# Attention prologues of a four-block Flamingo kernel: order of loads and queries, bias cleaned per pair, two PSUM banks

## The reference

```
x = x + tanh(g_xattn[i]) * attention_i(layernorm(x), ctx)
q = norm_x @ Wq.T (+ bq);  k = ctx @ Wk.T (+ bk);  v = ctx @ Wv.T (+ bv)
first attention:  q, k, v = nan_clamp(...)      # NaN -> 0, +inf -> 1e4, -inf -> -1e4
                  bias = clip(nan_clamp(bias), -1e4, 1e4)      # (1, 16, 56, 1500), same for all sequences
                  logits = q.k / sqrt(8) + bias; where mask == 0: -1e4; softmax; @ v; @ Wo.T + bo
second attention: softmax(q.k / sqrt(8)) @ v @ Wo.T             # no biases, no mask
fourth attention: softmax(q.k / sqrt(8) - 1e6 * mask) @ v @ Wo.T + bo
```

## Time and profile before

| | |
|---|---|
| median of 3 runs | 6163.29 us |
| profiled execution | 6152.64 us, span 6150.5 us, mean granted clock 0.936 |
| busy in the span | PE 86%, VectorE 73%, ScalarE 52%, GpSimd 30% |
| first attention, its first DMA to its first VectorE scores | 19.88 to 163.91 us |
| second attention, its first DMA to the matmul on the context of sequence 2 | 1646.79 to 1738.40 us |
| fourth attention, the same | 4962.67 to 5056.78 us |

### The profile page before, as it was taken

The page is one execution under the profiler, slowest core; times in us unless marked ns, Lnnn a source line. Parts: engine busy times, 40 slices in busy tenths (PEclk is TensorE's granted clock), DMA queues, the critical chain, the costliest instruction groups (busy, mean ns, idle before and its releaser), DMA issues. The chain is left out here.

```text
span 6150.5 us, 133121 instructions
## 1 busy us (share of the span) xinstructions
PE 5287.2 (86%) x51447; PEld 3802.1 (62%) x51447; DVE 4466.4 (73%) x9168; ACT 3193.4 (52%) x6024; POOL 1844.2 (30%) x1456
## 2 busy tenths in 40 slices
PE   1888989888669999989839999999999749999997
PEld 1777777777258888877824444444444427888885
DVE  6898898986357777763457777777777547777776
ACT  0666666666246666652224444444444216666663
POOL 4777676772022222211001111111111022222220
PEclk6999999999689999999969999999999869999998
DMA  4555565553167777743010000000000048888981
GB/s 107 124 131 126 127 129 125 131 125 80 37 122 140 140 140 139 140 81 115 24 31 21 16 15 15 15 15 15 15 15 10 7 91 151 163 161 161 161 155 30
DMA packets 368544, 545.53 MB, mean 89 GB/s; under 512 B 115780, under 2 KB 248006, under 8 KB 367606
## 3 DMA queue, kind: packets, MB, share of 16 engines
q1 hardware_dynamic: 365894, 533.81, 42.9%
q0 software_dynamic: 2048, 3.67, 0.2%
HBM read 413.45 MB, written 123.90 MB: 87 GB/s over the span
## 5 line engine op out<-in xcount | busy, mean ns | idle before, releaser
L653 DVE CUSTOM_DVE_ANT_0 attn_logits<-attn_scores,attn_shift 112x750 f32<-112x750 f32 x1024 | 944.9, 932 | 440.3 <-PE attn_scores L457 440.0
L569 ACT ACTIVATE attn_probs_t<-attn_pt 125x448 f32<-125x448 f32 x1536 | 829.6, 541 | 581.7 <-PE attn_pt L472 561.1
L472 PEld LDWEIGHTS attn_pt<-ident,attn_logits 112*125 112x125 f32 x6144 | 851.6, 189 | 179.7 <-issue 92.8
L472 PE MATMUL attn_pt<-ident,attn_logits 112*125 112x112 f32 x6144 | 920.7, 273 | 26.4 <-ACT attn_logits L560 24.8
L2246 PE MATMUL attn2k_pk<-attn_wk,attn2k_cn_t 128*125 128x512 f32 x1536 | 738.8, 603 | 53.0 <-ACT attn2k_cn_t L2317 36.7
L2257 PE MATMUL attn2k_pg<-attn2k_kn,attn2k_cn 125*128 125x512 f32 x1536 | 725.0, 594 | 6.0 <-ACT attn2k_gram L2325 3.9
L2412 DVE TENSOR_REDUCE attn2k_ss<-attn2k_sq 125x16 f32<-125x1024 f32 x384 | 466.9, 1216 | 257.7 <-ACT attn2k_sq L2354 257.6
L386 POOL CAST attn_k_parts<-xn_t 128x500 bf16<-128x500 f32 x192 | 199.3, 1038 | 1422.6 <-DVE xn_t L623 1422.6
L2354 ACT ACTIVATE attn2k_sq<-attn2k_pk 125x1024 f32<-125x1024 f32 x384 | 391.5, 1019 | 324.8 <-PE attn2k_pk L2246 324.6
L1165 ACT ACTIVATE attn_probs_t<-attn_pt 125x448 f32<-125x448 f32 x768 | 413.8, 539 | 275.0 <-PE attn_pt L1053 273.0
L2246 PEld LDWEIGHTS attn2k_pk<-attn_wk,attn2k_cn_t 128*125 128x125 f32 x1536 | 273.1, 187 | 416.7 <-issue 320.8
(11 more groups left out here) (363 smaller groups left out, 10434.9 us busy)
## 6 DMA issues: line engine op xcount, KB each, us to landing
attn_k_packed<-k_scratch SPq DMA_DIRECT2D x384, 375.0 KB, 6.4
attn_k_packed<-k_scratch SPq DMA_DIRECT2D x384, 187.5 KB, 4.4
k_scratch<-attn_k_parts SPq DMA_DIRECT2D x64, 1125.0 KB, 7.6
attn_ctx_t<-in_ctx_t SPq DMA_DIRECT2D x64, 750.0 KB, 7.4
k_scratch<-attn_k_parts SPq DMA_DIRECT2D x96, 375.0 KB, 3.7
attn_ctx_t<-in_ctx_t SPq DMA_DIRECT2D x96, 250.0 KB, 4.1
attn2k_ctx<-in_ctx SPq DMA_DIRECT2D x32, 750.0 KB
attn_mask_in<-in_mask SPq DMA_DIRECT2D x192, 109.4 KB
```

Of the source, the lines that this page charges most:

```text
L472: last = pe.transpose(pt[(3 * at + t) % 2][0:KC, (c % 4) * PAIR:(c % 4 + 1) * PAIR], logits[:, at % 3, c * KC:(c + 1) * KC], g.ident[0:PAI ...
L569: act.activation(probs_t[0:KC, p // 4, 4 * t:4 * t + 4, (p % 4) * PAIR:(p % 4 + 1) * PAIR], pt[(3 * at + t) % 2][0:KC, 0:QUAD].rearrange(" ...
L653: dve.tensor_tensor_reduce(out=logits[:, at % 3, cols].rearrange("p (b k) -> p b k", b=2), in0=scores[h][0:PAIR, :, 0:QTR], in1=shift[:, n ...
```

## The change

In all three attentions:

- The constants are in three groups with a semaphore each: wq and bq (`wq_in`), wk, wv, bk, bv (`wkv_in`), the rest (`const_in`). TensorE's and GpSimd's first waits are for the first group, TensorE waits for the second before the keys and for the rest before `sums(0)`; GpSimd before `blocks(0)`.
- SP stores the query parts and issues the query loads ahead of the key stores and loads.

In `turned_attention`: the prologue's keys and values alternate between the banks `side` and `po`; VectorE's four query operations stand between the three `keep` of sequence 0; the first key load is twelve DMAs, the six of the first four pairs under a semaphore of their own; context 2 stays behind the key loads of sequence 1.

In `masked_attention`: the bias comes in eight DMAs, and each pair is cleaned with two clamps and an add in place of not_equal, predicated copy and clamp. Pairs 0 to 5 are cleaned between `finite` and `take` of sequence 0's six pieces, pairs 6 and 7 between the marks. Both halves of the key loads of sequence 0 stand ahead of the masks 1 and 2. The value stand-ins of sequence 1 are made by VectorE (`guard_values`), and GpSimd's first guard of sequence 2 waits for v_ready 6.

```diff
 turned_attention
+        def bank(n, i):
+            return po if n < 2 and i % 2 else side
...
                 load_ctx(0)
+                for dst, src in consts:
+                    sp.dma_start(dst[:], src).then_inc(const_in, 16)
                 load_ctx(1)
                 if add:
                     load_mask(0)
                     load_mask(1)
-                pack_keys(0)
                 sp.wait_ge(q_split, 4)
                 sp.dma_start(a["q_scratch"].rearrange("a f t -> f a t"), q_parts).then_inc(q_stored, 16)
+                store_keys(0)
                 sp.wait_ge(q_stored, 16)
                 load_queries(0)
+                load_first_keys()
                 load_queries(1)
-                pack_keys(1)
+                store_keys(1)
+                load_keys(1)
                 load_ctx(2)
...
+                def emptied(n, i):
+                    if 6 * n + i >= 2:
+                        m, j = divmod(6 * n + i - 2, 6)
+                        pe.wait_ge(rest_ready if j < 3 else v_ready, 3 * m + j % 3 + 1)
...
-                dve.wait_ge(const_in, nconst)
                 for n in (0, 1):
                     for i in range(3):
+                        if n == 0:
+                            split_queries(i)
                         keep(n, i)
+                    if n == 0:
+                        split_queries(3)
                     for b in range(3):
                         hold_values(n, b)
-                    if n == 0:
-                        split_queries()
 masked_attention
                 for i in range(3):
                     load_ctx(0, i)
+                sp.dma_start(a["x_scratch"], g.x[:]).then_inc(x_away, 16)
+                load_bias(0)
+                for dst, src in consts:
+                    sp.dma_start(dst, src).then_inc(const_in, 16)
                 load_mask(0, 0)
-                sp.dma_start(bias[:], a["bias"]).then_inc(bias_in, 16)
+                for p in range(1, HP):
+                    load_bias(p)
+                sp.wait_ge(q_split, 4)
+                sp.wait_ge(x_away, 16)
+                sp.dma_start(a["q_scratch"].rearrange("a f t -> f a t"), q_parts).then_inc(q_stored, 16)
+                sp.wait_ge(q_stored, 16)
+                load_queries(0)
+                load_queries(1)
                 for i in range(3):
                     store_keys(0, i)
                 for i in range(3):
                     load_ctx(1, i)
                 load_keys(0, 0, range(NPART))
+                load_keys(0, 1, range(NPART))
                 load_mask(0, 1)
...
                 load_mask(0, 2)
...
+                def clean_bias(p):
+                    at, low = bias[:, p, :], logits[p % 2]
+                    dve.wait_ge(bias_in[p], 16)
+                    dve.tensor_scalar(low, at, 0.0, MASKED, ALU.min, ALU.max).then_inc(clean_steps, 1)
+                    dve.wait_ge(clean_steps, 3 * p + 1)
+                    dve.tensor_scalar(at, at, 0.0, -MASKED, ALU.max, ALU.min).then_inc(clean_steps, 1)
+                    dve.wait_ge(clean_steps, 3 * p + 2)
+                    dve.tensor_tensor(at, at, low, ALU.add).then_inc(clean_steps, 1)
+                    dve.wait_ge(clean_steps, 3 * p + 3)
...
+                def guard_values(n, b):
+                    done = 3 * (6 * n + b + 3)
+                    raw, to = as_v(raw_v[:, (3 * n + b + 3) % 2, :]), v_columns(n, b)
+                    low = as_v(q_below[0:KC, 0:512])
+                    dve.wait_ge(raw_v_ready, 3 * n + b + 1)
+                    dve.wait_ge(rough_steps, done)
+                    dve.tensor_scalar(low, raw, 0.0, MASKED, ALU.min, ALU.max).then_inc(rough_steps, 1)
+                    dve.tensor_scalar(to, raw, 0.0, -MASKED, ALU.max, ALU.min).then_inc(rough_steps, 1)
+                    dve.wait_ge(rough_steps, done + 2)
+                    dve.tensor_tensor(to, to, low, ALU.add).then_inc(rough_steps, 1)
...
                 for n in (0, 1):
                     for i in range(3):
                         finite(n, i)
+                        if n == 0:
+                            clean_bias(i)
                         take(n, i)
                     for b in range(3):
                         keep_values(n, b)
                         finite(n, b + 3)
+                        if n == 0:
+                            clean_bias(b + 3)
+                        else:
+                            guard_values(n, b)
                         take(n, b + 3)
                     if n == 0:
-                        for i in range(3):
-                            mark(0, i)
-                        clean_bias()
+                        mark(0, 0)
+                        clean_bias(6)
+                        mark(0, 1)
+                        clean_bias(7)
+                        mark(0, 2)
                         floors(0)
```

More of the change, by code:

```diff
@@ L339, in pack_keys, with load_first_keys @@
                                      scratch[part].rearrange("(p r) k -> r p k", r=16)).then_inc(k_in[n % 2], 16)
+                def load_first_keys():
+                    sp.wait_ge(k_stored, 16)
+                    for h, landed in enumerate((k_in_first, k_in[0])):
+                        for i, part in enumerate(K_PART):
+                            sp.dma_start(k_packed[16 * i:16 * i + 16, 0, 4 * h:4 * h + 4, :],
+                                         a["k_scratch"][0][part].rearrange("(p r) k -> r p k", r=16)[
+                                             :, 4 * h:4 * h + 4, :]).then_inc(landed, 16)
+                for dst, src in first:
+                    sp.dma_start(dst[:], src).then_inc(wq_in, 16)
+                for dst, src in second:
+                    sp.dma_start(dst[:], src).then_inc(wkv_in, 16)
                 load_ctx(0)
+                for dst, src in consts:
+                    sp.dma_start(dst[:], src).then_inc(const_in, 16)
                 load_ctx(1)
@@ L363, in _ @@
                 if w["bq"] is None:
-                    for t in (bq, bk, bo, bv):
+                    pool.memset(bq[:], 0.0)
+                    for t in (bk, bo, bv):
                         pool.memset(t[:], 0.0)
@@ L766, in masked_attention @@
         po, side = r.ps("po", [128, 512]), r.ps("side", [128, 512])
-        (x_away, const_in, bias_in, ones_ready, clean_steps, q_turned, q_ready, q_guarded, q_split, q_stored, q_in_even,
+        bias_in = [r.sem(f"bias_in{p}") for p in range(HP)]
+        (x_away, wq_in, wkv_in, const_in, ones_ready, clean_steps, q_turned, q_ready, q_guarded, q_split, q_stored, q_in_even,
          q_in_odd, blocks_ready, ctx_in0, ctx_in1, ctx_in2, k_turned, raw_k_ready, rough_steps, rough_ready, k_ready,
@@ L939, in guard @@
                         pool.wait_ge(q_guarded, Q_CLEAN)
+                    if n == 2 and i == 0:
+                        pool.wait_ge(v_ready, 6)
                     pool.tensor_scalar(low, raw, 0.0, MASKED, ALU.min, ALU.max).then_inc(rough_steps, 1)
```

145 lines of the change are left out of this document (76 added, 69 removed).

## The result

The change took the kernel from 6164.57 us to 6066.53 us (medians of four runs each), a ratio of 0.984 with a 95% interval of 0.982 to 0.986. The forecast was 6103 us, its range 6083 to 6126: right in direction, and 36 us short. So of the 98.0 us between the medians, 84.7 lie between the two traces and 13.3 are these two offsets.

What follows compares the result with a forecast made beforehand. No engine is saturated; chains of waits and DMAs in three attention prologues set the time. Savings of 26, 16 and 18 us, 60 in all, from 6152.64 give 6092.6, for the median 6103 us; range 6083 to 6126.

Steps and rivals of the forecast that it cites:

- First attention: Prologue of the first attention: first scores on VectorE at 138 instead of 163.9, saving 26 us.
- GpSimd's value guard: First attention, sequence 0: about 4.1 us from value to stand-in, less than a bias piece, so VectorE's waits vanish.
- the query store at no cost: First attention: query store and loads ahead of key stores cost nothing, or 3 us if the bias drains later.
- Second attention: Its prologue: earlier key loads and a shorter DMA chain to sequence 2's context save 16 us.
- Fourth attention: Its prologue: the same shorter DMA chain and an earlier start save 18 us.
- Nothing else changes: Loops: no instruction is added, they keep their pace, so only what the prologues save counts, 60 us.
- Rival 4: Attention loops settle in another, slower rhythm over some 92 sequences: 6268 us, or 6186 at half; chance 0.04.
- The median from one execution: Whole kernel: profiled execution lay 10.65 us under the median, so 6092.6 for it became 6103 for the median.
- The rule that I weighed: VectorE and GpSimd's shared port pair as exclusive lock; expected lengthening of a sixth to a quarter, under a whole GpSimd operation.
- rival 1: First attention, sequence 0: VectorE and GpSimd serialise, about 55 us against 44, gain 12 less, time 6115; chance 0.12.

Runs made afterwards that it cites:

- E9: Changed kernel, but bias pieces 0 to 5 cleaned behind sequence 0 instead of between its steps: 0.9867 of before, 6080.04 us; first scores at 149.34.
- E11: Changed kernel, but second and fourth attention split queries behind sequence 0's pieces and store and load them behind the first keys, as before: 0.9891 of before.
- E12: Changed kernel, but key and value products of the first two sequences of second and fourth attention go to one bank again: 0.9860 of before.
- E1: Kernel before with 24 more satisfied waits (12 instructions) at the start of VectorE's program in the first attention, nothing else: 0.9978 of before.
- E3: Changed kernel with `turned_attention` as before, so only the first attention is changed: 0.9916 of before.
- E4: Changed kernel with `masked_attention` as before, so only the second and fourth attention are changed: 0.9939 of before.
- E2: Changed kernel with 488 more satisfied VectorE waits (244 instructions) ahead of the third attention, 256 instructions more than before in all: 0.9886 of before.
- E6: Changed kernel with the context of sequence 2 loaded right behind the first keys in second and fourth attention: 0.9776 of before, 6025.88 us.

## Why the prediction was short

Taken by its own steps.

**First attention: right in its sum, wrong in one of its signs.** Queries on VectorE at 28.8 (forecast 29.4), through them at 43.0 (43.6), sequence 0 done at 89.9 (88), first scores at 136.1 (138), gain 27.8 (26). The pieces in company took 4.2 to 5.2 us, 4.6 in the mean (4.5). GpSimd was to be awaited nowhere in sequence 0; VectorE waited for it three times, 1.2 us each, 3.5 in all, where before it was 11.1. The mis-sized term is GpSimd's value guard: 4.1 us in the forecast, as it took beside an idle VectorE, and 5.7 (83.44 to 89.12) beside the bias pieces. The 3.5 us more than cover the 2.6 by which sequence 0 was longer than forecast (47.0 for 44.4). The mask landed at 100.5 (101.5); the wait was 5.1 and not 9, since VectorE came to it later and the pair before it began behind a slow mark. Sequence 1 took 29.0 us (29.3). That I had the query store at no cost was right only through its cover: E9 shows 12.3 us when the bias pieces are taken away, where I had written at most 3.

**Second attention: right, 18.0 for 16.** Start 3.5 (3); key loads 18.6 after the first key matmul (17.8); the chain behind them 46.2 us (48.3) where it was 63.2. E11 gives the part that the new order of the queries has in it, some 10 us; E12 gives the banks 0.6. The earlier start has 3.5; what the remaining 4 are made of was not tried. **Fourth attention: 22.5 for 18.** Start 6.4 instead of 5.0, and a chain of 45.4 where it was 63.6; E11 gives the order of the queries 9.8 us there and E12 the banks 2.6.

**Nothing else changes: this step failed.** The sum assumed that what a prologue saves is all there is, as no instruction of a loop was touched. The missing term is the third attention: 18.0 us from first to last copy (1568.2 to 1550.3). The change puts 12 more instructions into VectorE's program ahead of that loop, and its body is 288 instructions long (both counted in the program, waits in pairs). E1 (12 more, nothing else) and E3 (12 more) have the gain, E4 (none) hasn't, E2 (256 more) loses it. What decides is the place of the loop's code: places 256 instructions apart behave alike, and 12 to 18 further on than before the stop is gone. No other place was tried, so a shorter period isn't ruled out. In the bad place each pass moves 5 more packets of instructions (74 against 11 packets in the stretch of the loop, over 13 passes), stops VectorE for 1.1 us, and lengthens the pass by 1.4. The Trainium skill, "Runtime: NRT & Kernel Launch", section "Instruction fetch mechanics", has the mechanism: instructions come in blocks of 256, most engines hold two of them, and a taken branch to a block outside of these has to wait for a fetch. By that rule 288 instructions fit two blocks or touch three depending on where they begin, which agrees with the four runs; but no trace shows where the blocks begin, so the place is shown as the cause and the blocks are the Trainium skill's explanation of it. The Trainium skill calls the plain crossing of a block "mostly hidden" and gives the branch no price; here a pass costs 1.4 us. Rival 4's doubt (the loops' pace moves) was the right question, but I asked it of the attention loops alone and only as a loss, while the row with the 13 stops stood in the profile of before.

**The median from one execution: the second failed step.** I carried the 10.65 us by which the profiled execution lay under the median of before over to the changed kernel. Its own lay 1.4 above. Executions of before spread over 16 to 25 us in three of the four sets (6157.67 to 6173.4; 6153.25 to 6174.09; 6180.89 to 6205.84) and, but for one stray, over 17 in the fourth, more than what I took for an offset. Without the third attention the traces give 67.4 us (68.3 of the prologues, less 4.7 in the first loop and the first feed-forward part, plus 3.8 in the small rows of the table); from the median of before, 6163.29, that is 6096, inside the range. The third attention's 17.0 takes it to 6079, and the offset's 12 (10.65 carried over where 1.4 of the other sign was true) to 6067.

**Small ones.** The first attention's loop lost 2.1 us: its sequences last 42.4 or 43.5 to 43.9 us, and of the long kind the changed kernel's trace has ten where before had eight. The first feed-forward part lost 2.6 to the later clock, which varies between executions as E12 shows. The attention loops' 31.29 for 31.37 to 31.46 us gave 2.4 in the second; its cause is open.

**The rule that I weighed.** I had called the lengthening of VectorE's operations beside GpSimd smaller than a whole GpSimd operation. For single operations the traces now show more: in E9 GpSimd's query blocks run from 85.47 for 2.10 us, to 87.57, and VectorE's clamp beside them takes 2.40 us instead of 0.94, ending 0.8 after them.

```profile
85.47 2.10 POOL L973 TENSOR_TENSOR attn_q_blocks<-x_sb,attn_row_head 96x896 bf16<-96x896 bf16 x1 [0.24 <-POOL attn_v L1000]
```

```profile
85.96 2.40 DVE L1313 TENSOR_SCALAR attn_logits<-attn_bias 112x1500 f32<-112x1500 f32 x1
...
91.13 0.94 DVE L1313 TENSOR_SCALAR attn_logits<-attn_bias 112x1500 f32<-112x1500 f32 x1
```

The changed kernel's mark at 89.92 shows the same (1.88 instead of 0.42). It goes the other way too: GpSimd's addition, the last of the three operations of a value guard, takes 2.19 us beside VectorE's bias pieces and ends 1.0 after VectorE's addition (86.37 to 88.09), where it took 1.18 before.

```profile
86.93 2.19 POOL L1000 TENSOR_TENSOR attn_v<-attn_v,y_t 125x512 f32<-125x512 f32 x1
```

```profile
79.41 1.18 POOL L943 TENSOR_TENSOR attn_v<-attn_v,y_t 125x512 f32<-125x512 f32 x1
```

The Trainium skill's page "SBUF — State Buffer", section "SBUF: two separate sides", lets the second comer wait for the whole of the first one's operation, where VectorE's has two SBUF inputs or is in a two-port mode. The addition agrees; the clamp and the mark agree too, if they are in such a mode, which no trace shows. VectorE's own additions of two tensors (1.72 to 2.00) don't show it: this one ended 0.3 us after the GpSimd operation beside it and not 1.7.

```profile
45.69 2.56 POOL L998 TENSOR_SCALAR attn_clean_late<-xn_t 128x500 f32<-128x500 f32 x1
```

```profile
46.56 1.99 DVE L1317 TENSOR_TENSOR attn_bias<-attn_bias,attn_logits 112x1500 f32<-112x1500 f32 x1
```

Over sequence 0 all of this came to 3.5 us of waits and a stretch 2.6 us longer than forecast, not to rival 1's 12.

## What to carry to other kernels

Before you forecast, look in the profile for stops with the reason "issue" at the start of a loop's pass: here they depended on where the loop's code lies, so that an edit ahead of it that adds or removes instructions on that engine could switch them on or off; and when you compare variants, keep the count of instructions ahead of such loops equal, or the comparison measures the place too. A long stand for a load is first a question of that load's place in its queue: E6 moved one line and gained 40 us. An edit costs nothing only as long as its cover is there; name the cover, and when an experiment takes it away, expect the full transit and not the few us of work.

## What the runs showed of the hardware that I had not expected

- A loop of 288 VectorE instructions costs 1.4 us more per pass in one place than 12 instructions further on, and 256 instructions further it costs it again (E1, E2).
- The granted clock came back to 1.00 for good about 41 us into the first feed-forward part in one execution and 71 us in another with the same code there; in the second TensorE was busy for 43.5 of the 44.3 us before the rise. The difference was 15 us of the kernel's time, as large as many changes.
- On one chip the second feed-forward part took 30 us longer in all four kernels traced there; its cause is open, and the stops of VectorE for its own instructions there (16 us in E1, 63 in E2) don't follow the part's length (398.2, 399.4).
- GpSimd's operations are lengthened by VectorE's as well: a value guard of three operations took 5.7 us instead of 4.0.
